# First mixture of experts: results stored in slot order, gathered by token and weighted at the sum; rows loaded once

## The reference

```python
def _moe_forward(hidden_states, g, wt, wg, w_gate, w_up, w_down, sw_gate, sw_up, sw_down):
    ...
    scores = jax.nn.softmax(logits, axis=-1)
    topk_w, topk_idx = jax.lax.top_k(scores, K)                      # K = 2 of E = 8
    topk_w = topk_w / (topk_w.sum(-1, keepdims=True) + 1e-20)
    gp = _leaky(jnp.einsum('th,ehm->etm', x, w_gate))
    up = jnp.einsum('th,ehm->etm', x, w_up)
    y_all = jnp.einsum('etm,emh->eth', gp * up, w_down)
    y_sel = y_all[topk_idx, jnp.arange(T)[:, None], :]
    y = (y_sel * topk_w[..., None]).sum(1).reshape(b, s, h)
    p = _leaky(hidden_states @ sw_gate) * (hidden_states @ sw_up) @ sw_down
    y = y + p
...
x = x + _L0_attn_ref(_L0_cond_ref(x, cond_64, ...), ...)             # mixture, then attention 1
x = x + _L0_ffn_ref(_L0_cond2_ref(x, ...), ...)                      # attention 2, mixture 2
```

## Time and profile before

| | |
|---|---|
| three runs | 1680.83, 1683.24, 1689.78 us; median 1683.24 |
| span of the profiled execution | 1682.6 us |
| PE | 1368.7 us busy (81%) |
| VectorE | 1127.8 us (67%) |
| ACT | 815.6 us (48%) |
| POOL | 979.7 us (58%) |
| DMA, all queues | 281 MB, mean 167 GB/s |

### The profile page before, as it was taken

One profiled execution on the slowest core, in us unless ns is written; L12 is line 12 of the kernel. 1 busy time (PEld: TensorE's weight loads), 2 busy tenths in 40 slices (PEclk: granted clock), 3 DMA queues, 4 the chain that ended last, 5 costly groups with the idle time before them and its releaser, 6 DMA issues. The chain is left out here.

```text
span 1682.6 us, 34680 instructions
## 1 busy us (share of the span) xinstructions
PE 1368.7 (81%) x11604; PEld 1090.4 (65%) x11605; DVE 1127.8 (67%) x2697; ACT 815.6 (48%) x1587; POOL 979.7 (58%) x922
## 2 busy tenths in 40 slices
PE   6978986788787899999999999870398888878881
PEld 3768983555564577777777777650387877767771
DVE  6675783998774556978878797882144456656675
ACT  3334542444442455665756556440266655545551
POOL 4577775656652111556474554777177776666674
PEclk9999997999999899999999999985699989989996
DMA  9987662789970000111121111287566688888875
GB/s 283 291 261 226 188 202 50 230 230 304 257 208 24 5 1 2 46 57 68 44 80 48 68 58 46 87 296 207 182 192 190 201 274 272 279 264 268 267 234 196
DMA packets 193524, 281.23 MB, mean 167 GB/s; under 512 B 28515, under 2 KB 160240, under 8 KB 190582
## 3 DMA queue, kind: packets, MB, share of 16 engines
q1 hardware_dynamic: 145446, 155.12, 32.8%
q0 software_dynamic: 34560, 84.30, 14.2%
q10 hardware_dynamic: 13392, 40.11, 7.2%
HBM read 137.66 MB, written 152.25 MB: 172 GB/s over the span
## 5 line engine op out<-in xcount | busy, mean ns | idle before, releaser
L2394 POOL DMA_INDIRECT y_rows<-se_ys,se_yidx x320 | 321.2, 1004 | 157.7 <-issue 116.4
L1554 POOL DMA_INDIRECT x_slots<-wide,a_sidx x256 | 257.9, 1007 | 76.2 <-issue 71.0
L1541 POOL TENSOR_TENSOR flat<-flat,a_rs 128x512 f32<-128x512 f32 x64 | 69.9, 1093 | 240.0 <-DVE a_rs L2036 239.6
L2435 PE MATMUL ps<-ident,se_xs 128*128 128x128 f32 x640 | 92.8, 293 | 132.5 <-DMA se_xs<-x_slots 114.0
L2435 PEld LDWEIGHTS ps<-ident,se_xs 128*128 128x128 f32 x640 | 78.0, 151 | 152.6 <-issue 149.2
L2446 PE MATMUL ps<-se_xsT,se_up 128*128 128x128 f32 x1280 | 167.0, 287 | 0.0
L2446 PEld LDWEIGHTS ps<-se_xsT,se_up 128*128 128x128 f32 x1280 | 161.0, 204 | 0.1
L2542 DVE TENSOR_SCALAR se_ys<-ps,se_tail 128x256 f32<-128x256 f32 x160 | 70.0, 479 | 128.8 <-DMA y_rows<-se_ys,se_yidx 107.5
L2468 ACT COPY se_up<-w_up 128x256 f32 x320 | 106.0, 403 | 102.9 <-issue 102.6
L2420 PE MATMUL ps<-wide,se_hT 128*128 x640 | 152.0, 380 | 3.1 <-DVE se_hT L2533 3.0
L2420 PEld LDWEIGHTS ps<-wide,se_hT 128*128 128x128 f32 x640 | 116.0, 191 | 16.4 <-issue 4.0
(11 more groups left out here) (367 smaller groups left out, 3449.9 us busy)
## 6 DMA issues: line engine op xcount, KB each, us to landing
x_slots<-wide SPq DMA_DIRECT2D x50, 1032.0 KB, 14.2
se_xs<-x_slots SPq DMA_DIRECT2D x80, 516.0 KB, 4.8
se_got<-y_rows ACTq DMA_DIRECT2D x56, 512.0 KB, 5.4
wide<-x_slots SPq DMA_DIRECT2D x20, 516.0 KB, 5.0
e_xr<-in_x SPq DMA_DIRECT2D x16, 512.0 KB, 6.6
w_up<-in_up SPq DMA_DIRECT2D x8, 1024.0 KB, 18.3
wide<-in_down SPq DMA_DIRECT2D x5, 1024.0 KB, 10.6
y_rows<-se_ys,se_yidx POOLq DMA_INDIRECT x320
```

Of the source, the lines that this page charges most:

```text
L1541: pool.tensor_tensor(pn[:, m % 2].rearrange("p j h k -> p h j k"), sc[:, m % 2, :, :, 0:S], rs[:, m % 2].rearrange("p (h j) -> p h j", h=2 ...
L1554: pool.indirect_dma_start(out=x_slots, out_offset=bass.IndirectOffsetOnAxis(ap=sidx[:, r % 2, t, k_:k_ + 1], axis=0), in_=stage[:, t, k_, ...
L2394: pool.indirect_dma_start(out=y_rows, out_offset=bass.IndirectOffsetOnAxis(ap=yidx[:, (w - 2) % TR, b:b + 1], axis=0), in_=ys[:, w % 2, b, ...
L2435: last = pe.transpose(ps[:, b // 2, (b % 2 * C + c) * P:(b % 2 * C + c + 1) * P], xs[:, w % XR, b, c * P:(c + 1) * P], ident[:])
```

## The change

- A slot is 256 wide (`D`). The columns of token number and weight, the copies that fill and read them, and the ring `tail_i`, `tail_w` are gone.
- Slots of a group lie together: slot number s becomes group, partition, block in place of group, block, partition, so that a partition's four rows are contiguous. VectorE computes this with five more instructions on the slot numbers (128x32).
- Rows of x are loaded once; `xr` holds four parts of four tiles, and each row is sent from there to its two slots. SP's order changes: parts 0 to 3 are loaded around the clearing of the first half and the features, parts 4 to 7 behind the clearing of the second; then the bias, the attention's weights and the groups.
- Results are copied without a scale and stored by SP in slot order, one DMA per group (`store_slots`, behind `load_slots(g + 5)` in SP's list).
- POOL gathers by token: two indirect DMAs per tile, 32 for the first half behind the sends of `first_experts`, and 32 in slots 1 to 16 of the attention's loop.
- VectorE's `add_rows` multiplies by the weight as it adds: per tile two multiply-adds of 128x256; in the attention one slot later than before. Slot numbers and weights are kept at the end of `wide`.

```diff
-        x1_slots = [nc.dram_tensor(f"x1_slots{beta}", (EB * P, ROW), F32).ap() for beta in range(2)]
-        y1_rows = [nc.dram_tensor(f"y1_rows{beta}", (TB * P * K1, D), F32).ap() for beta in range(2)]
-        y1_tiles = [rows.rearrange("(t p k) d -> p t k d", p=P, k=K1) for rows in y1_rows]
+        x1_slots = [nc.dram_tensor(f"x1_slots{beta}", (EB * P, D), F32).ap() for beta in range(2)]
+        y1_slots = [nc.dram_tensor(f"y1_slots{beta}", (EB * P, D), F32).ap() for beta in range(2)]
         y1_out = [sem(f"y1_out{w}") for w in range(YR)]
         got1_in, added1 = [sem("got1_in0"), sem("got1_in1")], sem("added1")
-
-        def returned(w, groups):
-
-            return len(range(w, groups, YR)) * GB * 16
+        KEPT = E2 * D - 4 * TB * K1
+        kept = [wide[:, KEPT + i * TB * K1:KEPT + (i + 1) * TB * K1] for i in range(4)]
+        sidx1 = [kept[2 * beta].bitcast(I32).rearrange("p (t k) -> p t k", t=TB) for beta in range(2)]
+        wk1 = [kept[2 * beta + 1].rearrange("p (t k) -> p t k", t=TB) for beta in range(2)]
+
+        def slots_stored(w, groups):
+
+            return len(range(w, groups, YR)) * 16
+
+        def gather_tile(pool, beta, t, to, landed):
+
+            for k in range(K1):
+                pool.indirect_dma_start(
+                    out=to[:, k, :], out_offset=None, in_=y1_slots[beta],
+                    in_offset=bass.IndirectOffsetOnAxis(ap=sidx1[beta][:, t, k:k + 1], axis=0)).then_inc(landed, 16)
 
         ITEMS = 8
         kpd = wide[:, 0:4096].rearrange("p (b c s h k) -> p b c s h k", b=2, c=C, s=SPB, h=2)
...
-                        eng.dma_start(slots[g], pad_row.unsqueeze(1).to_broadcast([P, 8, ROW])).then_inc(pad1[beta], 16)
+                        eng.dma_start(slots[g], pad_row[:, 0:D].unsqueeze(1).to_broadcast([P, 8, D])).then_inc(pad1[beta], 16)
...
-                        wait(sp, sent1[q % 2], q // 2 * TPB * K1 * 16)
-                        for k in range(K1):
-                            sp.dma_start(xr[:, q % 2 * TPB:(q % 2 + 1) * TPB, k, 0:D],
-                                         x.rearrange("(t p) d -> p t d", p=P)[:, q * TPB:(q + 1) * TPB, :]
-                                         ).then_inc(xr_in[q % 2], 16)
+                        wait(sp, sent1[q // 2 % 2], q // QR * 2 * TPB * K1 * 16)
+                        sp.dma_start(xr[:, q % QR * TPB:(q % QR + 1) * TPB, :],
+                                     x.rearrange("(t p) d -> p t d", p=P)[:, q * TPB:(q + 1) * TPB, :]
+                                     ).then_inc(xr_in[q // 2 % 2], 16)
...
                     for q in range(N1 - 2):
                         load_expert(q)
                     load_rows(0)
-                    sp.wait_ge(pad_step, 2)
+                    sp.wait_ge(pad_step, 1)
                     clear_slots(sp, 0, range(EB // 8))
+                    load_rows(1)
                     load_features(1)
-                    load_rows(1)
+                    load_rows(2)
+                    load_rows(3)
                     load_expert(N1 - 2)
                     load_expert(N1 - 1)
                     sp.wait_ge(rel_sb, len(runs))
                     sp.dma_start(rel_rows.rearrange("q h r -> h q r"),
                                  reld.unsqueeze(1).to_broadcast([H1, S, REL])).then_inc(rel_out, 16)
-                    clear_slots(sp, 1, (0, 1))
-                    load_rows(2)
-                    clear_slots(sp, 1, (2, 3))
-                    load_rows(3)
-                    clear_slots(sp, 1, (4,))
+                    clear_slots(sp, 1, range(EB // 8))
+                    for q in range(QR, 2 * QR):
+                        load_rows(q)
                     sp.wait_ge(rel_out, 16)
                     for s in range(2):
                         diag = bass.AP(rel_rows.tensor, S - 1, [[H1 * REL - 1, S], [REL, H1], [1, S]])
                         sp.dma_start(bias1[s * S:(s + 1) * S], diag).then_inc(bias1_in, 16)
-                    load_rows(4)
-                    load_rows(5)
                     for dst, src in ((wq, wqT), (wk, wkT), (wv, wvT), (wo, woT)):
                         sp.dma_start(dst, src.rearrange("(c p) n -> p c n", p=P)).then_inc(a1_in, 16)
 
-                    xv = [slots.rearrange("(g b p) d -> g p b d", p=P, b=GB) for slots in x1_slots]
+                    xv = [slots.rearrange("(g p b) d -> g p b d", p=P, b=GB) for slots in x1_slots]
+                    yv = [slots.rearrange("(g p b) d -> g p b d", p=P, b=GB) for slots in y1_slots]
...
-                    def load_returned(q):
-                        if q == 0:
-                            for w in range(YR):
-                                sp.wait_ge(y1_out[w], returned(w, GPB))
-                        wait(sp, added1, q - 1)
-                        for k in range(K1):
-                            sp.dma_start(xr[:, q % 2 * TPB:(q % 2 + 1) * TPB, k, 0:D],
-                                         y1_tiles[0][:, q * TPB:(q + 1) * TPB, k, :]
-                                         ).then_inc(got1_in[q % 2], 16)
-
-                    for g in range(NG1):
-                        load_slots(g)
-                        if g in (1, 3):
-                            load_rows(6 + g // 2)
-                        if NG1 - 4 <= g < NG1 - 2:
-                            load_returned(g - (NG1 - 4))
-                    load_returned(2)
-                    load_returned(3)
+                    def store_slots(g):
+                        sp.wait_ge(ya_done, NB + g + 1)
+                        sp.wait_ge(yb_done, g + 1)
+                        sp.dma_start(yv[g // GPB][g % GPB], ys[:, g % YR]).then_inc(y1_out[g % YR], 16)
+
+                    for g in range(NG1 + XS):
+                        if g < NG1:
+                            load_slots(g)
+                        if g >= XS:
+                            store_slots(g - XS)
...
-                        beta, mine = q // 4, slice(q % 2 * TPB, (q % 2 + 1) * TPB)
-                        pool.wait_ge(xr_in[q % 2], (q // 2 + 1) * K1 * 16)
-                        pool.tensor_copy(xr[:, mine, :, D:D + 1].bitcast(I32).rearrange("p t k o -> p t (k o)"),
-                                         ids1[:, q * TPB:(q + 1) * TPB, :])
-                        pool.tensor_copy(xr[:, mine, :, D + 1:ROW].rearrange("p t k o -> p t (k o)"),
-                                         wk1[beta][:, q % 4 * TPB:(q % 4 + 1) * TPB, :]).then_inc(tailed, 1)
-                        pool.wait_ge(tailed, q + 1)
-                        pool.nop(nofuse=True)
+                        beta = q // QR
+                        pool.wait_ge(xr_in[q // 2 % 2], (beta + 1) * 2 * 16)
                         for t in range(TPB):
                             for k in range(K1):
                                 pool.indirect_dma_start(
                                     out=x1_slots[beta],
-                                    out_offset=bass.IndirectOffsetOnAxis(ap=sidx1[beta][:, q % 4 * TPB + t, k:k + 1], axis=0),
-                                    in_=xr[:, q % 2 * TPB + t, k, :], in_offset=None).then_inc(sent1[q % 2], 16)
+                                    out_offset=bass.IndirectOffsetOnAxis(ap=sidx1[beta][:, q % QR * TPB + t, k:k + 1], axis=0),
+                                    in_=xr[:, q % QR * TPB + t, :], in_offset=None).then_inc(sent1[q // 2 % 2], 16)
+
+                    def gather(q):
+                        pool.wait_ge(sent1[q % 2], 2 * 2 * TPB * K1 * 16)
+                        wait(pool, added1, q - 1)
+                        for t in range(TPB):
+                            gather_tile(pool, 0, q * TPB + t, got1[:, q % 2, t], got1_in[q % 2])
 
...
-                    pool.wait_ge(made, CONSTANTS + 1)
-                    pool.tensor_copy(pad_row[:, D:D + 1], pad_i[:]).then_inc(pad_step, 1)
-                    for g in range(NG1):
-                        pool.wait_ge(ya_done, NB + g + 1)
-                        pool.wait_ge(yb_done, g + 1)
-                        pool.nop(nofuse=True)
-                        for b in range(GB):
-                            pool.indirect_dma_start(
-                                out=y1_rows[g // GPB],
-                                out_offset=bass.IndirectOffsetOnAxis(ap=tail_i[:, g % TR1, b:b + 1], axis=0),
-                                in_=ys[g % YR][:, b, :], in_offset=None, bounds_check=TB * P * K1 - 1, oob_is_err=False
-                                ).then_inc(y1_out[g % YR], 16)
+                    for w in range(YR):
+                        pool.wait_ge(y1_out[w], slots_stored(w, GPB))
+                    for q in range(QR):
+                        gather(q)
...
-                            wait(act, y1_out[g % YR], returned(g % YR, g))
-                            for b in range(2):
-                                last = act.activation(ys[g % YR][:, b, :], ps[:, 4, b * D:(b + 1) * D], ACT.Copy,
```

(59 more changed lines are left out.)

48 lines of the change are left out of this document (21 added, 27 removed).

## The result

Five executions of the changed kernel took 1690.87 to 1698.74 us, median 1696.51; the kernel before, 1680.83 to 1689.78, median 1682.39. The ratio is 1.0073 (95% interval 1.0041 to 1.0105): 12 us slower, where 1687.2 was predicted and 1696.5 measured. The profiled execution has a span of 1696.7 us.

A forecast was written before the change was run, and what follows sets the result against it. Bounds: the DMA engines up to about 110 us, PE in the groups, VectorE in the first attention. Terms 2.0 - 1.5 - 6.2 + 7.2 + 2.5 = +4.0 us on 1683.24 gave 1687.2 us, range 1672 to 1703.

The forecast's parts named there:

- the forecast's own range: Whole kernel: the forecast case, apart from the rivals, 1678 to 1692 us, chance 0.5.
- First stage, slot numbers +2.0: Ahead of the groups: five more small VectorE instructions, 1.0 us, twice, delay the subtraction PE waits for; +2.0 us.
- Collision -1.5: First stage: POOL's two weight subtractions meet VectorE's two-input subtractions near 86 us and cost less than before; -1.5 us.
- Start of the groups -6.2: Group 2's slot load no longer queues behind a load of rows; 5.3 us of wait and 0.9 of slow clock go.
- End of the groups +7.2: Before PE's keys and queries: gathers of part 2 wait for the first `add_rows`, delaying the hT copy; +7.2 us.
- the border costs what it did: End of the groups: the border to the next block takes no longer than before, POOL and VectorE through no later than PE.
- First attention +2.5: First attention: two gathers per slot on POOL fit, with some lateness, causal bias and slow landings; +2.5 us (-7.8 to +14).
- Second adds of 0.5 where 2.0 stood: First attention, a sign of being right: VectorE's second adds take 0.5 us where 2.0 stood.
- Rival one: First attention: POOL becomes the bound through dearer gathers, 1698 to 1708 us; chance 0.2.
- Rival three: Start of the groups: SP's new order makes the first slot load late, 1693 to 1698 us; chance 0.1.
- Rival two: Whole kernel: VectorE's waits for POOL go and the gathers hide, so it is faster, 1671 us; chance 0.2.
- VectorE's two-input operations beside POOL: First attention: VectorE's two-input adds wait for POOL's running tile operation; one such wait, 2.01 us, falls to 0.48.

The follow-up runs named there:

- rest_old_place: The changed kernel, but POOL's two last weight subtractions wait until the second half's slot numbers are known; ratio 1.0090 to the kernel before.
- half_gathers: The changed kernel, but in the first attention only the first of a token's two rows is gathered and added twice; ratio 1.0083 to the kernel before.
- combined: The changed kernel with POOL's last weight subtractions in VectorE's idle time, old slot order, early sums in pieces, first attention's gathers a slot earlier; ratio 0.9993.
- the last edit here: combined, with seven loads of very small pieces issued in block 5 of the first attention and ACT's preparations in slot 24, not 8; ratio 1.0004.

## Why the prediction was right or wrong

The direction and the range were right (slower, 1672 to 1703). The centre was 9 us low, the time lies outside the forecast's own range (1678 to 1692), and two of the terms were far off. That the time stayed within the whole range is partly luck: at slot 31 the changed kernel was 22.2 us behind, which would make 1705, and 8 us came back in work that the change doesn't touch.

- *First stage, slot numbers +2.0*: the operations cost what was said (0.17 to 0.19 us each, 1.0 us in all for the second half). What failed is that the term ended there. Together with the collision they made PE's wait behind them grow from 1.5 to 3.7 us, its clock fell, and taking the operations out brought the groups 4.6 to 7.5 us forward. The sum's terms for this stage count no clock that falls behind a wait.
- *Collision -1.5*: wrong in sign. POOL reached it at 88.1, 2 us behind the forecast, but it cost 4.0 us, not less than the 3.2 of before, ahead of the tighter place. Together the two terms gave +0.5; the first transposes came 6.8 to 9.6 us late.
- *Start of the groups -6.2*: the mechanism was right, in both kernels; 3.6 to 5.5 us measured in the changed kernel's code, the low end where the clock was low in groups 0 and 1 (108.0 us for all the groups in the changed kernel, 106.1 in rest_old_place, which had full clock in both). In the kernel before the move of the load gave 3.9 us.
- *End of the groups +7.2*: the chain was right link by link. From the last transposes to the copy of hT the changed kernel takes 27.0 us and the kernel before 19.9, that is +7.1. But the border moved by 3.6 only, and the step that failed is that the border costs what it did. It does not follow PE's last product: in the versions of the changed kernel it stands 4.0 to 8.1 us behind that, but 8.3 us behind POOL's last key spread in each of them, and 7.6 us in the kernel before. There POOL, with its scatters until 257.9 and two key spreads, ended at 261.7, 0.7 us after PE. In the changed kernel it ended at 270.8, 4.1 us before PE. So PE's end moved by 7.8 us from the last transposes, POOL's by 3.0.
- *First attention +2.5*: +12.1 measured from slot 0 to slot 31, inside its bounds (-7.8 to +14) and far from the value taken. POOL's part held: 0.96 us a gather and 0.30 between, a period of 31.9 us (31 to 33 forecast), POOL busy 27.2 of 31.9 us, with 1.8 of gaps ahead of the gathers. The step that failed is the landing. It was taken as 7.2 us, from scatters beside pad stores, and covered by two slots. Three of the four gathers of the first two tiles took 13.1 to 13.5 us, one 7.7, behind loads of 0.2 to 2 KB. The list of SP's issues gave a sign of it: in the kernel before two pairs of such loads hold SP for 6.5 and 9.2 us, while its first loads of returned rows are issued ahead of them.
- *"Second adds of 0.5 where 2.0 stood"*: mostly so (median 0.485, 32 sums 30.9 us against 32.2 before), with some up to 2.7.
- *Rival one* (POOL the bound): out, by half_gathers. *Rival three* (the first slot load late): out; PE waited for VectorE and its own clock. *Rival two* (faster): its ingredients, the start and the collision, were real; combined has them, and is level.
- *VectorE's two-input operations beside POOL*: the prediction took such a wait at one POOL operation. The runs show more: VectorE's operation waits for as many POOL tile operations as follow each other, 5.27 us for 1.22 across two of them and 6.13 for 1.00 across three. The Trainium skill ("SBUF — State Buffer", section "SBUF: two separate sides") describes a shared pair of ports that a VectorE operation with two SBUF inputs and a GpSimd (POOL) operation that reads SBUF can't hold at once. That VectorE stood while POOL's tile operations ran, in both of these traces, agrees with it.

What stays open: why slots 16 to 18 are 3.8 us longer, and the last 1100 us, in which executions of every version, the kernel before among them, differ by more than most of these edits are worth. Why the clock fell behind the 2.95 us wait in nine of the fourteen traces and not in the other five isn't shown either.

## What to carry to other kernels

A moved operation keeps its collisions: ask at its new place which two-input VectorE operation runs there, and how close PE is to standing still. A gather's landing must be read against what small-piece loads SP issues in the same stretch, not against the bytes. And where a wait goes, look who then arrives early at whom: the last edit here removed 4.9 us of wait and got 5.1 us of another.
